# A packed first chunk, a split last chunk in the second stage, and the layer norm's shift added by a transfer

## What is computed

```python
x = x + 0.5 * ffn(layernorm(x))
x = x + attention(layernorm(x))
x = x + 0.5 * ffn(layernorm(x))

def ffn(x):                                   # 9 experts, 64 hidden units each
    x_mixed = mix[0]*x[s-1] + mix[1]*x[s] + mix[2]*x[s+1]
    h = einsum('bsd,pdm->bspm', x_mixed, W1) + b1
    stacked = einsum('bspm,pmd->bspd', h, W2) + b2
    scores = tanh(x_mixed @ Wo1 + bo1) @ Wo2 + bo2
    weights = one_hot(argmax(scores, -1), 9)
    collapsed = einsum('bspd,bsp->bsd', stacked, weights)
    return layernorm_affine(x + collapsed, gamma, beta)
```

## Time and profile before

| | us |
|---|---|
| median of 3 runs | 1419.31 (1419.24 to 1419.68) |
| the profiled execution | 1418.93 |
| its span, first to last instruction | 1417.1 |
| PE busy in the span | 1329.5 (94%) |
| DVE busy | 1152.0 (81%) |
| ACT busy | 925.2 (65%) |
| GpSimd busy | 326.9 (23%) |

### The profile page before, as it was taken

The page is one execution under the profiler, slowest core; times in us unless marked ns, Lnnn a source line. Parts: engine busy times, 40 slices in busy tenths (PEclk is TensorE's granted clock), DMA queues, the critical chain, the costliest instruction groups (busy, mean ns, idle before and its releaser), DMA issues.

```text
span 1417.1 us, 24674 instructions
## 1 busy us (share of the span) xinstructions
PE 1329.5 (94%) x7700; PEld 770.8 (54%) x7700; DVE 1152.0 (81%) x2301; ACT 925.2 (65%) x1717; POOL 326.9 (23%) x396
## 2 busy tenths in 40 slices
PE   4999999988999999998998999999998879999997
PEld 2577776754445454544454455454544346777765
DVE  7899999887778787778877778787778777888876
ACT  6666776465666767565865666767575877766742
POOL 2344553450101000230030101000240003443443
PEclk9999999999999999999999999999999999999999
DMA  6165554440010000102000010000102212555544
GB/s 179 36 168 137 138 150 127 121 120 0 31 46 16 30 30 0 43 3 88 32 22 24 31 46 16 30 30 1 39 7 75 89 33 58 144 143 141 124 110 121
DMA packets 91498, 98.43 MB, mean 69 GB/s; under 512 B 9084, under 2 KB 87429, under 8 KB 91397
## 3 DMA queue, kind: packets, MB, share of 16 engines
q1 hardware_dynamic: 86932, 80.91, 19.3%
q0 software_dynamic: 4464, 16.25, 6.0%
HBM read 55.43 MB, written 25.46 MB: 57 GB/s over the span
## 4 chain that ended last, share of the span: by engine, by line
PE 73%; DVE 15%; ACT 7%; issue 4%; POOL 0%; DMA 0%; DVEq 0%; ACTq 0%; POOLq 0%; SPq 0%
PE PS L1827 64%; PE PS L1953 3%; PE PS L1835 3%; DVE R L1221 2%; DVE R L1215 2%; DVE run_max L1209 2%; PE PS L1924 2%; ACT R L1667 2%; ACT R L1671 1%; DVE x_st L905 1%; ACT R L1626 1%; DVE R L1016 1%; DVE st L816 1%; DVE R L1022 1%; PE PS L1933 1%
## 5 line engine op out<-in xcount | busy, mean ns | idle before, releaser
L1827 PE MATMUL PS<-R 128*128 128x512 f16 (+3 forms) x3456 | 719.9, 363 | 37.3 <-DVE R L1221 27.8
L1827 PEld LDWEIGHTS PS<-R 128*128 128x128 f16 (+1 forms) x3456 | 326.9, 98 | 397.0 <-DVE R L1221 54.9
L1221 DVE TENSOR_TENSOR R<-R 128x512 f16<-128x512 f32 (+3 forms) x288 | 189.2, 657 | 97.2 <-ACT R L1671 95.4
L1658 ACT ACTIVATE R<-PS 128x512 f32 (+5 forms) x288 | 160.4, 558 | 157.2 <-PE PS L1827 157.2
L1667 ACT ACTIVATE R<-R 128x512 f32<-128x512 f32 (+4 forms) x288 | 169.9, 590 | 57.1 <-DVE R L1215 56.3
L1827 PE MATMUL PS<-R,w_hi 128*128 128x512 f16 x636 | 193.5, 386 | 4.6 <-DVE R L866 2.5
L1827 PE MATMUL PS<-w_hi,R 128*128 128x256 f16 x1024 | 188.3, 273 | 3.3 <-DVE R L940 1.5
L1209 DVE TENSOR_TENSOR run_max<-run_max,R 128x512 f32<-128x512 f32 (+3 forms) x272 | 183.0, 673 | 8.4 <-DVE run_max L1209 1.7
L1671 ACT ACTIVATE R<-R 128x512 f16<-128x512 f32 (+3 forms) x288 | 171.7, 596 | 26.9 <-ACT R L1667 0.4
L1215 DVE TENSOR_TENSOR R<-R,max_row 128x512 f32<-128x512 f32 (+4 forms) x288 | 187.3, 650 | 0.5 <-ACT max_row L1735 0.5
L604 POOL TENSOR_SCALAR veps<-mv 128x4 f32<-128x4 f32 x48 | 14.9, 311 | 552.5 <-issue 328.3
(11 more groups left out here) (137 smaller groups left out, 1698.3 us busy)
## 6 DMA issues: line engine op xcount, KB each, us to landing
R<-x_scratch SPq DMA_DIRECT2D x48, 512.0 KB, 4.4
x_scratch<-R SPq DMA_DIRECT2D x32, 512.0 KB, 3.2
R<-R POOLq DMA_DIRECT2D x31, 512.0 KB, 4.6
R<-oh_scratch SPq DMA_DIRECT2D x32, 320.0 KB
R<-in_L_attn_x SPq DMA_DIRECT2D x16, 512.0 KB, 5.1
R<-oh_scratch SPq DMA_DIRECT2D x32, 256.0 KB
out<-R SPq DMA_DIRECT2D x15, 512.0 KB, 3.1
R<-in_L_ffn_W SPq DMA_DIRECT2D x2, 288.0 KB
```

Of the source, the lines that this page charges most:

```text
L1221: v.tensor_tensor(p_lo[:, i * TT + lo:(i + 1) * TT], pf[:, (i % 2) * TT + lo:(i % 2 + 1) * TT], p_hi[:, i * TT + lo:(i + 1) * TT], ALU.sub ...
L1658: a.activation(cols(ring, ring_m + i * TT + lo, TT - lo), ps_s[:, i, lo:], ACT.Abs, scale=1.0 / (QS * XS * D ** 0.5)).then_inc(abs_done, 1)
L1827: ins = t_.matmul(dst, w, xx, start=start and n == 0, stop=stop and n == last, skip_group_check=skip)
```

## The change

- **Chunk 0 is packed.** The bias b2 is loaded a second time, into rows 9 to 17 of chunk 0's weights, and the one-hot rows are written twice (`oh` is 2 x 9 wide, and 18 rows go to the mask). `hlo` of chunk 0 holds the low part of expert 0's units in rows 0 to 63 (DVE) and their high part again in rows 64 to 127 (ACT). PE multiplies it by `w2_twice`, which holds expert 0's high weights twice, and `hhi` by a `w2_lo` whose rows 0 to 8 hold b2's high part: two matmuls for each u, not three.
- **Chunk 4 of the second stage is split**, as the others are: three fp16 matmuls and not one fp32 matmul, for which ACT rounds it and DVE takes its remainder (group 2). The first stage keeps the fp32 matmul.
- **`beta` is added by an accumulating transfer** of GpSimd from the broadcast `beta_b`; it waits for the transfer before it of the same kind, and no longer for the masking.

```diff
+                load(w2_v[NP:2 * NP, 0, :], b2, w2_in)
...
-                    sp.dma_start(m[0:NP, 0, :], there).then_inc(mask_in[g % 2], 16)
+                    sp.dma_start(m[0:2 * NP, 0, :], there).then_inc(mask_in[g % 2], 16)
...
-                    if t < NTT - 1:
-                        pool.wait_ge(hm_done, HC * (k + 1) + 1)
-                    g.tensor_tensor(rows4(x_rows(t)), rows4(x_rows(t)),
-                                    beta_b[:, :].unsqueeze(1).to_broadcast([P, SUB, D]), ALU.add).then_inc(xb_done, 1)
+                    if k >= 1:
+                        pool.wait_ge(xb_done, 16 * k)
+                    g.dma_start(rows4(x_rows(t)), beta_b[:, :].unsqueeze(1).to_broadcast([P, SUB, D]),
+                                accum_op=ALU.add).then_inc(xb_done, 16)
...
                     dve.wait_ge(hhi_done, groups_before(ph, t) + i + 1)
+                    if c == 0:
+                        v.tensor_tensor(chunk(hlo, t, 0)[0:DM, :], masked_chunk(t, 0)[DM:P, :], chunk(hhi, t, 0)[DM:P, :],
+                                        ALU.subtract)
+                        c, n = 1, n - 1
...
+                def pair_weights():
+
+                    act.wait_ge(w2_ready, 1)
+                    a.activation(w2_twice[0:DM, :], w2_hi[DM:P, 0, :], ACT.Copy)
+                    a.activation(w2_twice[DM:P, :], w2_hi[DM:P, 0, :], ACT.Copy)
+                    a.activation(w2_lo[0:NP, 0, :], w2_hi[0:NP, 0, :], ACT.Copy).then_inc(w2_paired, 1)
...
                     a.activation(chunk(hhi, t, c, n), masked_chunk(t, c, n), ACT.Copy).then_inc(hhi_done, 1)
+                    if i == 0:
+                        a.activation(chunk(hlo, t, 0)[DM:P, :], masked_chunk(t, 0)[DM:P, :], ACT.Copy).then_inc(pair_done, 1)
...
                 masked_high(0, 1)
+                if ph == 1:
+                    masked_high(0, 2)
                 transposed(ph, 4)
...
+                def paired_product(dst, high, pair, u, start):
+
+                    t_.matmul(dst, cols(pair, u * P, P), w2_twice[:, :], start=start, stop=False, skip_group_check=True)
+                    return t_.matmul(dst, cols(high, u * P, P), w2_lo[:, 0, :], start=False, stop=False,
+                                     skip_group_check=True)
...
-            return c == LAST
+            return ph == 0 and c == LAST
```

More of the change, by code:

```diff
@@ L998, in route @@
                         dve.wait_ge(route_step, k + 4)
-                        v.tensor_tensor(oh[:, :, :], r_pr[:, :, :], r_top[:, :].unsqueeze(2).to_broadcast([P, SUB, NP]),
+                        v.tensor_tensor(oh[:, :, :, :], r_pr[:, :, :].unsqueeze(2).to_broadcast([P, SUB, 2, NP]),
+                                        r_top[:, :].unsqueeze(2).unsqueeze(3).to_broadcast([P, SUB, 2, NP]),
                                         ALU.is_equal).then_inc(oh_done, 1)
@@ L1488, in one_hot @@
                         act.wait_ge(oh_stored, 16 * g)
-                    a.activation(oh_t[:, :], ps_oh[0:NP, 0:TT], ACT.Copy, scale=1.0 / WS).then_inc(ohT_done, 1)
+                    a.activation(oh_t[:, :], ps_oh[0:2 * NP, 0:TT], ACT.Copy, scale=1.0 / WS).then_inc(ohT_done, 1)
+                def pair_weights():
[3 more added lines that the diff above has]
+                    a.activation(w2_lo[0:NP, 0, :], w2_hi[0:NP, 0, :], ACT.Copy).then_inc(w2_paired, 1)
                 def masked_high(t, i):
@@ L1597, in ffn @@
                     one_hot(1)
+                if ph == 0:
+                    pair_weights()
                 masked_high(0, 0)
                 masked_high(0, 1)
+                if ph == 1:
+                    masked_high(0, 2)
                 transposed(ph, 4)
@@ L1944, in path @@
                             pe.wait_ge(x2_done, SUB * NTT)
+                    if c == 0:
+                        pe.wait_ge(pair_done, g + 1)
                     if whole(ph, c):
@@ L1957, in path @@
                                                        (w2_hi[:, c, :], w2_lo[:, c, :]))],
-                                                c == 0 and u % 2 == 0, c == LAST, skip=True)
+                                                False, c == LAST, skip=True)
                     if c == HC - 1:
@@ L1964, in path_by_rows @@
                     pe.wait_ge(nT_done, g + 1)
-                    pe.wait_ge(hlo_done, groups_before(ph, t) + len(GROUPS) - 1)
+                    pe.wait_ge(hlo_done, groups_before(ph, t) + len(GROUPS))
                     pe.wait_ge(hm_done, HC * g + HC)
+                    pe.wait_ge(pair_done, g + 1)
                     for u in range(SUB):
                         dst = PS[:, ROW_BANKS[u], 0:D]
-                        for c in range(LAST):
+                        paired_product(dst, chunk(hhi, t, 0), chunk(hlo, t, 0), u, True)
+                        for c in range(1, LAST):
                             split_product(dst, [((cols(chunk(hhi, t, c), u * P, P), cols(chunk(hlo, t, c), u * P, P)),
                                                  (w2_hi[:, c, :], w2_lo[:, c, :]))],
-                                          c == 0, False, skip=True)
-                        t_.matmul(dst, cols(masked_chunk(t, LAST), u * P, P), w2_last[:, :], start=False, stop=True,
-                                  skip_group_check=True).then_inc(last_psum, 1)
+                                          False, False, skip=True)
+                        split_product(dst, [((cols(chunk(hhi, t, LAST), u * P, P), cols(chunk(hlo, t, LAST), u * P, P)),
+                                             (w2_hi[:, LAST, :], w2_lo[:, LAST, :]))],
+                                      False, True, skip=True).then_inc(last_psum, 1)
                 def turn(t):
```

30 lines of the change are left out of this document (20 added, 10 removed).

## The result

| | before | after |
|---|---|---|
| median of its runs, us | 1419.49 (6 runs, 1419.24 to 1420.01) | 1410.08 (6 runs, 1408.06 to 1414.13) |
| the profiled execution, us | 1418.93 | 1408.60 |
| its span, us | 1417.1 | 1406.5 |
| granted clock, mean | 0.988 | 0.987 |

The ratio of the medians is 0.9937, with a 95% interval of 0.9926 to 0.9947. The change gains 9.4 us in the median; 15.8 were predicted (1403.5, range 1400.5 to 1408.5), so the measured time lies above the range. Two things have to be explained. The profiled execution gained 10.3 us and not 15.8. And the executions of the changed kernel now lie up to 6 us apart, where those of the kernel before lay within 1 us. (Measured again beside the experiments, in series of 9 to 23 executions, the kernel before spread over 1.9 to 3.1 us, so part of that contrast is the small number of runs.)

The account below looks back on a forecast made before the run. PE's matmuls were taken to bound ordinary turns, with DVE close behind. Gains of 6.1 us in the first stage and 9.7 in the second made 15.8, from 1418.93 to 1403.1 profiled, 1403.5 in the median; range 1400.5 to 1408.5.

Parts of the forecast that it names:

- Ordinary turns, what PE saves: PE-bound turns of both stages: 0.44 us saved a turn in the first (to 15.11), 0.86 in the second (to 14.69).
- What DVE pays: First-stage turns: splitting the remainder of chunks 0 and 1 into two 512-wide instructions costs DVE 0.24 us.
- the 0.30 that was free: First-stage turns: slack before DVE's result that path(t, 0) waits for; 0.24 would be used and 0.06 left.
- Rival 1: DVE becomes the bound in first-stage turns, its 64-partition instruction costing over 0.30; likely 1405 to 1408 us; chance 14%.
- the 0.3 forecast: First-stage turns 11 and 12, DVE-bound: pays 2 x 0.28, gets back 0.23 of waiting for PE, a loss of 0.3.
- The stall of turn 14: DVE's remainder waits for GpSimd's SBUF read; without tensor_tensor the stall goes, 1.2 us gained in the first stage.
- The transfer, cost 0 on the path: Beta transfers in each turn: about 3 us of the DMA engines, 11.7 fitting in 15.1; SyncE behind none of it.
- The second beta transfer of turn 14, count 0: It waits for the first to land, but GpSimd's next step waits for DVE's scaling anyway; counted 0.
- Start of the second stage, +1.74: PE's route(2) waits for the tanh, now behind chunk 4's rounding; PE starts 1.74 us later, and all of it stays.
- The prologue, count 0, at worst 1.2: First stage's prologue: ACT's pair_weights falls where the first remainder waits for DVE's maskings; counted 0, 1.2 us at worst.
- The attention, only starts earlier: The attention, some 850 us between the stages, is not touched by the change and only starts earlier.
- a wait that I didn't see: Anywhere in the kernel: an unforeseen wait brings the time up to 1411 us; chance 4%.

Follow-up runs that it names:

- e6: Changed kernel, but GpSimd issues the beta transfer of tile t+1 at the end of turn t, so turn 14 no longer has two; median 1416.72 us.
- e7: As e6, with ACT's copy of the pair and rounding of chunk 4 moved behind scores(2) at the second stage's start; median 1414.34 us.
- e2: Kernel before with only the beta transfers in place of GpSimd's tensor_tensor, chunks as before; median 1418.90 us.
- e10: As e9, with ACT's pair copy and chunk 4 rounding also moved behind scores(2) at the second stage's start; median 1407.24 us.
- e11: Changed kernel with only ACT's pair copy and chunk 4 rounding moved behind scores(2) at the second stage's start; median 1408.84 us.
- e12: As e10, but DVE takes the moments of tile 5 ahead of the last remainder of tile 0; median 1405.42 us.
- e3: Changed kernel, but at the second stage's start ACT rounds chunk 4 of tile 0 behind scores(2); pair copy not moved; median 1407.53 us.
- e8: Changed kernel with the second stage's last chunk left as one fp32 chunk; packing and transfers stay; median 1414.20 us.
- e9: Changed kernel, but SyncE issues the 512 KB store of tile t-1's result behind the next turn's mask loads; median 1408.56 us.
- e1: Changed kernel with GpSimd's tensor_tensor adding beta again in place of the transfer; packed and split chunks stay; median 1421.04 us.
- e4: Changed kernel, but the beta transfer reads one 4 KB run in DRAM per partition, not four 1 KB runs of SBUF; median 1414.33 us.
- e5: The changed kernel itself, measured and profiled again with nothing altered; median 1410.19 us.

## Why the prediction missed, step by step

- *Ordinary turns, what PE saves.* Right: 15.11 and 14.70 against 15.11 and 14.69; 13 turns of the second stage gave 10.92 of 11.08.
- *What DVE pays.* Right in mechanism, 0.06 off in size. Timeline of DVE in the changed kernel:

```profile
241.66 1.22 DVE L870 TENSOR_TENSOR R<-R 128x1024 f16<-128x1024 f32 x1
242.91 0.69 DVE L1030 TENSOR_TENSOR R<-R 64x512 f16<-64x512 f32 x1
243.61 0.69 DVE L1033 TENSOR_TENSOR R<-R 128x512 f16<-128x512 f32 x1
244.22 0.74 DVE L1023 SCALAR_TENSOR_TENSOR R<-PS,b1c,R 128x512 f32<-128x512 f32 x1
```

  From L870 to L1023 it is 2.56, where two 1024-wide ones took 2.26: 0.30, not 0.24. The 64-partition instruction starts 0.03 after its forerunner's end, and the next one 0.01 after its own. That used up the 0.30 that was free, and PE still stayed the bound (busy for 15.11 of 15.11). Rival 1 did not happen; turns 11 and 12 lost the 0.3 forecast (the lead fell from 3.44 to 3.13).
- *The stall of turn 14.* It went in both stages (L1030 and L1033 take 0.69 each), and 1.2 was gained in the first, as forecast. The judgement that GpSimd's read was the cause is borne out by the run without the transfer. The step was still too small: it saw the stall only where it stood in the trace of before. The price of leaving GpSimd's tensor_tensor in, 11 us in the medians and 10.9 in the two stages of the traces, was hidden by the 1.08 that DVE waited for PE, cover which the change itself takes away.
- *The transfer, cost 0 on the path.* **This step failed**, the first of two. It asked whether the engines have room (8.7 + 3 of 15.1 us) and whether SyncE's queue stands behind the transfer, and took the answer to both for the answer to a third question: who is late when a small transfer must go there and back between two large ones. The runs showed in its place a cost of 1.6 us on the path: DVE's waits for the mask took 0.67 in turn 3 and 0.96 in turn 14 of the first stage, and moving SyncE's store out of the round trip gave them back (283.42 against 284.95). The size was off as well (3.8, not 3), which matters less.
- *The second beta transfer of turn 14, count 0.* The wait was there (5.11 in the second stage), and it is on the path. The chain that ended last runs through it:

```profile
1381.32 5.90 DMA R<-beta_b
...
1387.78 1.25 POOL R L641
1389.03 0.90 POOL R L651
```

  DVE's scaling, for which L651 also waits, ended 11.57 earlier than before (1388.26 against 1399.83), but L651 ends only 11.1 earlier (1389.93 against 1401.04): 0.5 went to issuing the second transfer. In e6 and e7, which have no such pair, the stretch from choice of turn 13 to the end is 37.7, where it is 38.0 in the changed kernel; 37.6 was due. So some 0.3 of the 0.39 in the last row of the table is this step's. DVE's wait of 2.7 for the mask, just before, is not on that chain.
- *Start of the second stage, +1.74.* The idle time was right (1.54 more), from two causes of which I had named one. **The price was half of what it cost**, and this is the other step that failed: it took the cost of an idle gap to be its length, and 1.67 more came from the granted clock. Three doses at this place show it: idle 0.77 and the clock stays at 1.00 (before, e2, e7, e10, e11, e12), 1.27 and it falls (e3, e8), 2.31 and it falls (after). The Trainium skill, TensorE: Matmul & The Clock Gate, "Part 1", says that the array's clock is gated to 1.2 GHz when PE has been idle and released by activity; the trace agrees, in the window of 0.50 behind route(2). The length of the gap alone does not settle it, though: in the attention of e10 PE stood still for 2.59 and then 1.27 us and the clock stayed at 1.00, while in e9, behind gaps of 2.60 and 1.12 at the same place, it was 0.50.
- *The prologue, count 0, at worst 1.2.* 0.73 was lost; 0.51 of it was there at PE's matmuls before pair_weights runs (32.12 against 31.61), so that is not its price. Nor can it be put down to the change: in the traces with the changed kernel's prologue, choice of turn 0 comes anywhere from 53.79 (e8) to 55.13 (e6), and at 54.26 in the kernel before.
- *The attention, only starts earlier.* It was 0.56 longer (843.22 from the last result of the first stage to the first matmuls of the second, 842.66 before). That is chance, too: with the same code there it took 842.3 to 845.1 in the fourteen traces.

So of the 5.2, the mask made 1.6, the clock 1.7, prologue and attention 1.3 by chance, and the end 0.4, most of it by the second transfer; the rest is small. The measured median was 1.5 above the profiled execution besides. The range left half of such costs out: a wait that I didn't see had 4%, up to 1411, and that is where the time fell.

**What stays open** is what made single executions of 1411 to 1414 us. Two things vary by microseconds between traces. One is the waits for the mask (one to six in the changed kernel and the variants that leave the transfer in its place, 2.5 to 11.3 us in all). The other is the clock level at the start of a group of products in the attention. One group of 42 matmuls tells the traces apart: in e1, e4, e6, e9 and e12 it took 9.9 us and the attention 844.8 to 845.1; in the nine others it took 7.3 to 8.0 and the attention 842.3 to 843.7. The chain has the group's products in one row; first e9, then e10, whose code is the same there:

```profile
743.84 9.91 PE PS L1859 x42
```

```profile
744.82 7.32 PE PS L1864 x42
```

So the clock in the attention alone moves an execution by some 2 us, without any change of code. The granted clock over the whole run points the same way in e1: five executions with 0.982 took 1421.0 to 1422.2 and five with 0.985 or 0.986 took 1417.9 to 1419.8 (one with 0.988 took 1421.1). But it isn't all: the changed kernel's slowest (1414.13) had 0.986, and its two fastest 0.987. No trace of a slow execution of the changed kernel itself was at hand, so the shares are not known.

## What to carry to other kernels

When you remove work from the engine that bounds, its neighbours' waits for it shrink too, and these waits may be what keeps two other engines from meeting on a shared resource: shift the neighbours' rows by the saving and look again for overlaps. A small transfer with a round trip in it can be on the path before the DMA engines are full (here at 0.84), so cost every added transfer by what it delays, not by the share that it takes. Price an idle gap of TensorE by the clock behind it as well as by its length. And before you credit an edit with 1 or 2 us, look at the stretch that it changes: the untouched stretches of these traces differ by more than that.

## What the runs showed of the hardware that I had not expected

- An idle gap of 1.27 us cost another 1.7 us by half the granted clock (route(2) to choice took 7.46 in e3 and 5.80 in e12; the 6.06 of e11 holds a wait of 0.22 for the one-hot), while one of 0.77 in the same place cost nothing beyond its length. Behind 2.31 us it was no more: 7.45. Behind 2.60, in e5, it was 8.82, with the clock at 0.50 from the start.
- The clock need not fall in the gap itself: in the changed kernel it was 1.00 while PE stood still for 2.31 us and 0.98 in the first 0.9 us of work behind it, and only then 0.50. In e5 it was 0.90 over the last 2.7 us before route(2) and 0.50 from there on.
- The same 42 matmuls of the attention, in kernels whose code there is identical, took 7.32 us with the granted clock at 1.00 (e10) or 9.91 with it at 0.50 for the first 5.2 us (e9), behind idle gaps of nearly the same lengths.
- An accumulating transfer of 512 KB took 3.8 us of 16 engines with 528 packets and 3.0 with 144, and the cheaper one, which read DRAM, went with a later one-hot (86.1 against 67.3 us of waits).
- A store of 18 KB took 6.09 us behind three transfers of 512 KB. Without beta's transfer, in e1, a store of 18 KB at the same place let SyncE go on after 3.5. In an ordinary turn, SyncE waited 1.37 for 9 KB (issued at 148.60, went on at 149.97) and 1.37 for 18 KB (149.93 and 151.30 in e1).
